# Pairwise attention pooling: one block per loop body on TensorE, a ring of three PSUM slots with x in it, and x scaled by GpSimd

## What is computed

```python
row, col = np.triu_indices(F, k=1)
ip = x[:, row, :] * x[:, col, :]
hidden = jax.nn.relu(jnp.einsum('bpd,da->bpa', ip, W_w) + b_w)
logits = jnp.einsum('bpa,a->bp', hidden, W_h) + b_h[0]
a = jax.nn.softmax(logits, axis=1)[:, :, None]
pooled = jnp.sum(a * ip, axis=1)
return pooled @ W_p + b_p
```

## Time and profile before

| | |
|---|---|
| median of 3 runs | 1325.57 us (1322.91 to 1327.94) |
| the profiled execution, own time | 1334.73 us |
| its span, first to last instruction | 1332.9 us |
| mean granted TensorE clock | 0.951 of 2.4 GHz |
| TensorE / VectorE / ScalarE / GpSimd busy | 87% / 70% / 71% / 22% |
| TensorE's instructions | 25856 matmuls, 25856 weight loads |
| mean data rate of the DMAs | 36 GB/s |

### The profile page before, as it was taken

One profiled execution on the slowest core, in us unless ns is written; L12 is line 12 of the kernel. 1 busy time (PEld: TensorE's weight loads), 2 busy tenths in 40 slices (PEclk: granted clock), 3 DMA queues, 4 the chain that ended last, 5 costly groups with the idle time before them and its releaser, 6 DMA issues.

```text
span 1332.9 us, 60251 instructions
## 1 busy us (share of the span) xinstructions
PE 1156.1 (87%) x25856; PEld 517.9 (39%) x25856; DVE 934.6 (70%) x484; ACT 951.3 (71%) x1123; POOL 286.6 (22%) x263
## 2 busy tenths in 40 slices
PE   7988979789787997979979889797997979979984
PEld 3433434334343443434433344333443434434432
DVE  8686667866678675876867767577686776867870
ACT  5776767767677686767857678576785767857873
POOL 3131221212122131221302213032130221312220
PEclk9998989999899998989989899898998989989998
DMA  3142132312423123241222412324122241412312
GB/s 51 30 46 34 28 41 35 47 28 28 41 39 40 31 31 39 39 48 22 33 36 39 49 21 32 37 39 49 21 37 34 37 49 21 48 30 33 46 20 22
DMA packets 333436, 47.63 MB, mean 36 GB/s; under 512 B 333280, under 2 KB 333280, under 8 KB 333280
## 3 DMA queue, kind: packets, MB, share of 16 engines
q1 hardware_dynamic: 331264, 45.16, 26.6%
q10 hardware_dynamic: 2016, 0.01, 0.1%
HBM read 26.59 MB, written 18.54 MB: 34 GB/s over the span
## 4 chain that ended last, share of the span: by engine, by line
PE 85%; issue 12%; ACT 1%; DMA 1%; SPq 1%; ACTq 0%; DVE 0%; DVEq 0%
PE z L481 52%; PE logits L501 25%; PE z L452 4%; PE x_cols L439 3%; ACT hidden L356 1%; PE logits L491 1%; DMA values<-gram 0%; DMA gram<-gram_out 0%; DMA bp_col<-in_L_rec_b_p_dram 0%; SPq L188 0%; ACTq L398 0%; SPq L176 0%; SPq L174 0%; ACTq L392 0%; ACTq L393 0%
## 5 line engine op out<-in xcount | busy, mean ns | idle before, releaser
L356 ACT ACTIVATE hidden<-z,b_col 128x988 f32<-128x988 f32 x768 | 815.1, 1083 | 319.2 <-PE z L481 308.2
L277 DVE TENSOR_TENSOR prod<-x_wide 128x2964 f32<-128x2964 f32 (+1 forms) x257 | 821.7, 3242 | 96.7 <-PE z L481 89.1
L481 PE MATMUL z<-prod,w_tiles 64*32 64x494 f32 x12288 | 833.9, 590 | 4.6 <-ACT hidden L356 2.8
L501 PE MATMUL logits<-hidden,head_w 64*32 64x371 f32 (+1 forms) x8192 | 489.6, 491 | 33.9 <-issue 33.4
L236 POOL COPY head_w<-head_cols 128x64 f32<-128x64 f32 x252 | 277.0, 1099 | 1007.8 <-PE logits L501 1004.6
L481 PEld LDWEIGHTS z<-prod,w_tiles 64*32 64x32 f32 x12288 | 234.0, 108 | 325.6 <-issue 254.1
L501 PEld LDWEIGHTS logits<-hidden,head_w 64*32 64x32 f32 x8192 | 197.7, 109 | 279.3 <-issue 271.8
L259 DVE COPY x_wide<-x_cols 128x624 f32<-128x624 f32 (+1 forms) x64 | 51.4, 804 | 246.1 <-PE x_cols L439 244.1
L340 ACT ACTIVATE x_scaled<-x_wide,wp_col 128x156 f32<-128x156 f32 x256 | 105.9, 414 | 1.2 <-DMA bp_col<-in_L_rec_b_p_dram 1.2
L491 PE MATMUL logits<-w_tiles 64*32 64x2 f32 x256 | 8.3, 185 | 96.3 <-issue 96.3
L452 PE MATMUL z<-x_wide,x_scaled 64*39 64x39 f32 x4096 | 56.5, 202 | 20.6 <-issue 20.6
(11 more groups left out here) (16 smaller groups left out, 14.6 us busy)
## 6 DMA issues: line engine op xcount, KB each, us to landing
x_rows<-in_r_x_dram SPq DMA_DIRECT2D x128, 156.0 KB
gram<-gram_out SPq DMA_DIRECT2D x256, 47.5 KB
gram<-gram_out SPq DMA_DIRECT2D x256, 23.2 KB
values<-gram SPq DMA_DIRECT2D x128, 46.3 KB, 3.6
w_tiles<-in_L_rec_W_w_dram SPq DMA_DIRECT2D x4, 16.0 KB, 2.5
head_cols<-in_L_rec_W_h_dram ACTq DMA_DIRECT2D x4, 0.2 KB, 3.8
out_dram<-y_all SPq DMA_DIRECT2D x4, 1.0 KB, 3.4
out_dram<-y_all ACTq DMA_DIRECT2D x4, 1.0 KB, 4.3
```

The lines of the kernel that those rows point to most:

```text
L277: nc.vector.tensor_tensor(out, one, other, ALU.mult).then_inc(ready, 1)
L356: nc.scalar.activation(hidden[:, i, :, CHUNK * k:CHUNK * (k + 1)], z[:, (slot + item(j)) % 2, :, 0:CHUNK], ACT.Relu, bias=b_col[:, 0:1]).t ...
L481: last = nc.tensor.matmul(z[col:col + TILE, at, b, 0:CHUNK], w_tiles[row:row + D, col:col + TILE], prod[row:row + D, i, first:first + CHUN ...
L501: last = nc.tensor.matmul(logits[TILE * q:TILE * (q + 1), part, 0:cols], head_w[row:row + A, e, b, :], hidden[row:row + A, e, b, first:fir ...
```

## The change

**TensorE's loops.** `two_blocks` is gone. The inner loop's body is one block and runs four times in a group; behind the outer loop, a loop of one block runs twice, and the last two blocks are written out.

**PSUM.** `z` has three slots. Besides the 12 chunks and the gram matrices, the transposed x goes through the ring too: 14 items in fixed slots that are the same in each block (`SLOT`, `X_SLOT`, `GRAM_SLOT`), and `EARLIER` says for each chunk which item it takes the slot from. `x_cols` is gone.

**SBUF.** `x_rows` and `x_wide` have one slot instead of two. So `load(v)` waits until x of v - 1 has been transposed, and the spread of a block waits for the gram matrices of the block before, which read `x_wide`.

**Scaling.** GpSimd scales x in one instruction a block, ahead of the block's four head copies; ScalarE no longer does.

**Start.** SP loads both halves of x first, then the weights; it also takes the six small DMAs for the head weights and the two scalars from ScalarE's queue, and `load(1)` comes behind them.

The diff, cut to its core:

```diff
-    SLOTS = 2
+    SLOT = (2, 1, 0, 2, 1, 0, 0, 1, 0, 2, 1, 0)
+    EARLIER = (9, 10, 11, 0, 1, 2, 5, "gram", 6, "x", 7, 8)
+    X_SLOT, GRAM_SLOT, FIRST_X_SLOT = 2, 1, 0
+    BEFORE_X, BEFORE_GRAM = 3, 4
...
-        x_rows = sb("x_rows", [ROWS, SLOTS, 2 * ROW_DUOS, D])
-        x_wide = sb("x_wide", [P, SLOTS, BLOCK_DUOS, WIDE])
+        x_rows = sb("x_rows", [ROWS, 2 * ROW_DUOS, D])
+        x_wide = sb("x_wide", [P, BLOCK_DUOS, WIDE])
...
-        z = ps("z", [P, 2, 2, BANK])
+        z = ps("z", [P, 3, 2, BANK])
         logits = ps("logits", [P, 2, BANK])
-        x_cols = ps("x_cols", [P, 2, BANK])
...
-            def load(v, slot):
+            def load(v):
+                sp.wait_ge(x_cols_ready, v + 1)
...
-                        sp.wait_ge(x_cols_ready, v + 2)
-                        load(v + 2, m % SLOTS)
+                        load(v + 2)
...
+            def scale_x(v):
+
+                pool.wait_ge(x_spread, 2 * (v + 1))
+                if v == 0:
+                    pool.wait_ge(act_spread, 2)
+                    pool.wait_ge(cols_loaded, 16 * N_COLS)
+                else:
+                    pool.wait_ge(z_ready, ITEMS * (v - 1) + CROSS_AT + 1)
+                nc.gpsimd.tensor_scalar(x_scaled[:, :, :], x_wide[:, :, 0:FIELDS], wp_col[:, 0:1], None,
+                                        ALU.mult).then_inc(x_scaled_ready, 1)
...
             for step in range(BLOCK_STEPS, STEPS):
+                if step % BLOCK_STEPS == 0:
+                    scale_x(step // BLOCK_STEPS)
                 place_heads(step)
...
-            def spread(v, slot, first=False):
+            def spread(v, first=False):
 
-                if not (isinstance(v, int) and v < SLOTS):
-                    dve.wait_ge(prod_ready, BLOCK_STEPS * (v - 1))
+                if not first:
+                    dve.wait_ge(prod_ready, BLOCK_STEPS * v)
+                    dve.wait_ge(z_ready, ITEMS * (v - 1) + CROSS_AT + 1)
                 dve.wait_ge(x_cols_ready, 1 if first else v + 2)
...
-                    if j == 1 and not (isinstance(v, int) and v == 0):
-                        scale_x(v, slot, 3)
-                    if more and j in (6, 7, 10):
-                        scale_x(v + 1, 1 - slot, (6, 7, 10).index(j))
...
+            def claim_slot(v, j, with_x):
+
+                earlier = EARLIER[j]
+                if earlier == "gram":
+                    pe.wait_ge(z_read, ITEMS * v + CROSS_AT + 1)
+                elif earlier == "x":
+                    if with_x:
+                        pe.wait_ge(x_spread, 2 * (v + 2))
+                elif earlier < j:
+                    pe.wait_ge(z_read, ITEMS * v + item(earlier) + 1)
...
-            def two_blocks(n):
-                block_work(2 * n, 0, n + 1)
-                block_work(2 * n + 1, 1, n + 2)
...
-                with pe.Fori(0, GROUP_BLOCKS // 2) as w:
-                    two_blocks(GROUP_BLOCKS // 2 * g + w)
+                with pe.Fori(0, GROUP_BLOCKS) as m:
+                    block_work(GROUP_BLOCKS * g + m)
...
-            two_blocks(BLOCKS // 2 - 2)
-            block_work(BLOCKS - 2, 0)
-            block_work(BLOCKS - 1, 1, following=False)
+            with pe.Fori(BLOCKS - GROUP_BLOCKS, BLOCKS - 2) as v:
+                block_work(v)
+            block_work(BLOCKS - 2, with_x=False)
+            block_work(BLOCKS - 1, following=False)
```

More of the change, by code:

```diff
@@ L147, in bass_pairwise_attention_pooling @@
         y_stored = sem("y_stored")
[L149 removed]
+        N_COLS = 4
+        N_SCALARS = 2
         GRAM_DMAS = 8
@@ L194, in _ @@
                     sp.dma_start(w_tiles[h * D:(h + 1) * D, c * A:(c + 1) * A], w_hidden).then_inc(w_loaded, 16)
-            sp.dma_start(x_rows[D:D + FIELDS, 0, :, :], x_rows_dram[1, :, 0, :, :]).then_inc(first_x_loaded[1], 16)
-            load(1, 1)
+            sp.wait_ge(zeroed, 1)
+            for h in range(2):
+                for b in range(2):
+                    at = GROUP_STEPS - 1 + GROUP_STEPS * (h ^ b)
+                    sp.dma_start(head_cols[h * D:(h + 1) * D, b, at:at + 1],
+                                 w_logit.rearrange("(a o) -> a o", o=1)).then_inc(head_cols_loaded, 16)
+            for col, scalar in ((bh_col, b_logit), (bp_col, b_out)):
+                sp.dma_start(col[:, :],
+                             scalar.rearrange("(a o) -> a o", o=1).broadcast_to((P, 1))).then_inc(scalars_loaded, 16)
+            load(1)
             def group(g, pairs, last=False):
@@ L279, in find_max @@
             def find_max(g):
+                if isinstance(g, int) and g == 0:
+                    dve.wait_ge(scalars_loaded, 16 * N_SCALARS)
                 dve.wait_ge(logits_done, GROUP_STEPS * (g + 1))
@@ L297, in pool_group, with block_work @@
                                         ALU.mult, ALU.add).then_inc(y_ready, 1)
-            def block_work(v, slot, pooled_group=None, ended=None, more=True):
-                multiply(v, slot, 0)
+            def block_work(v, pooled_group=None, ended=None, more=True):
+                multiply(v, 0)
                 if pooled_group is not None:
@@ L304, in block_work @@
                 for i in range(1, BLOCK_STEPS):
-                    multiply(v, slot, i)
+                    multiply(v, i)
                 if ended is not None:
@@ L334, in _, with rectify @@
         def _(act):
[L335 to L341, removed]
             def spread_first():
                 act.wait_ge(x_cols_ready, 2)
-                cols = x_cols[:, 1, 0:XCOLS].rearrange("p (q f) -> p q f", f=FIELDS)
-                wide = x_wide[:, 0, ROW_DUOS:BLOCK_DUOS, :]
+                cols = z[:, FIRST_X_SLOT, 1, 0:XCOLS].rearrange("p (q f) -> p q f", f=FIELDS)
+                wide = x_wide[:, ROW_DUOS:BLOCK_DUOS, :]
                 nc.scalar.copy(wide[:, :, 0:FIELDS], cols).then_inc(act_spread, 1)
                 nc.scalar.copy(wide[:, :, FIELDS:WIDE], cols[:, :, 0:OFFSETS]).then_inc(act_spread, 1)
-            def rectify(v, slot, j):
+            def rectify(v, j):
                 i, k = j // THIRDS, j % THIRDS
@@ L375, in exponentials, with block_work @@
                                      accum_out=exp_sum[:, :]).then_inc(logits_free, 1)
-            def block_work(v, slot, writes, ended=None, more=True):
+            def block_work(v, slot, writes, ended=None):
                 for j in range(CHUNKS):
-                    rectify(v, slot, j)
+                    rectify(v, j)
                     if j == CROSS_AT - 1:
@@ L425, in _ @@
                 v = BLOCKS - GROUP_BLOCKS + m
-                block_work(v, m % SLOTS, v // 2, ended=GROUPS - 2 if m == 0 else None, more=m < GROUP_BLOCKS - 1)
+                block_work(v, m % 2, v // 2, ended=GROUPS - 2 if m == 0 else None)
             exponentials(GROUPS - 1)
@@ L472, in hidden_layer @@
                     pe.wait_ge(prod_ready, BLOCK_STEPS * v + i + 1)
-                if not (isinstance(v, int) and v == 0 and j < 2):
-                    pe.wait_ge(z_read, ITEMS * v + item(j) - 1)
+                claim_slot(v, j, with_x)
                 nc.tensor.sem_inc(z_claimed, 1)
-                at = (slot + item(j)) % 2
                 for a in range(0, A, TILE):
```

142 lines of the change are left out of this document (64 added, 78 removed).

## The result

The changed kernel takes 1100.55 us (median of 4 runs, 1099.71 to 1101.29) against 1326.76 us (4 runs, 1322.91 to 1328.64): a ratio of 0.830, 95% interval 0.828 to 0.832.

The account below looks back on a forecast made before the run. TensorE's own time and its issue time (code fetches) bound the kernel. Sum 19.3 + 956.5 + 4.5 + 68.3 + 55.9 + 26.0 = 1130.5 us span, 1132 profiled, forecast 1128; range 1108 to 1190 us.

Parts of the forecast that it names:

- the profiled run: Profiled execution before lay 9.2 us above the median of the runs; half was taken off, 1132 to 1128 us.
- the fetches: TensorE's outer return reads its code again; a one-block body would not, saving 14.2 us in each of 14 groups.
- Three slots: Chunk gated by the reading three places before instead of two: gains nothing, as undisturbed blocks have TensorE busy 16.99 of 17.01 us.
- the stalls of a first pass: TensorE's first reading of code, with stalls and slow clock: 4.5 us kept in the first group, 6.4 at the end.
- the ring: Slots of z that chunks and x share: third slot gains nothing, new waits for x and its spread not on the path.
- the group's end: Opening of the logits between TensorE's groups: 0.27 us without a fetch, some 0.2 us of it on the chain.
- the scaling: Scaling x moves from ScalarE to GpSimd: worth 0, off the path; GpSimd's instruction taken as 1.0 us, bounds 0.81 and 2.3.
- The rival of GpSimd and VectorE: The two hinder each other, x_scaled or the spread comes late, TensorE waits 1 us a block: 1192 us, chance 0.09.
- the port: GpSimd's scaling may begin only after VectorE's first multiplication, done 3.2 + 1.0 us after the spread; needed some 14 us after.
- the outer return still misses: Rival: TensorE's outer return still fetches its code, 12.3 us at each of 14 returns, 172 in all: 1300 us, chance 0.07.
- every return fetches: Rival: TensorE's inner returns fetch too, 7.1 us for each of 46, plus 172 us: 1627 us, chance 0.03.
- The start: Load order and ScalarE's six DMAs before the first chunk: bounds -4 and +3 us, taken as -2.

Follow-up runs that it names:

- e2: Kernel before, with the opening of the logits done two more times ahead of TensorE's outer loop (64 instructions, executed once): 1134.2 us, ratio 0.861.
- e8: Changed kernel with two copies of the block in TensorE's inner body, shifted by 64 instructions: 1097.9 us, ratio 0.834 to the kernel before.
- e9: Kernel before, with the opening of the logits done six more times ahead of TensorE's outer loop (192 instructions, executed once): 1473.9 us, ratio 1.118.
- e4: Changed kernel, each chunk gated by the item two places before it, though it has three slots: 1127.9 us, ratio 0.857 to the kernel before.
- e6: Changed kernel with two copies of the block in TensorE's inner body and each chunk gated two items before: 1315.4 us, ratio 0.999 to the kernel before.
- e1: Changed kernel with two copies of the block in TensorE's inner body, run twice a group: 1241.8 us, ratio 0.944 to the kernel before.
- e3: Changed kernel with x scaled by ScalarE in four pieces between the chunks, not by GpSimd: 1099.8 us, ratio 0.834 to the kernel before.

## Why the prediction was right and wrong

| term, us | predicted | measured |
|---|---|---|
| to the first logit half | 19.3 | 18.9 |
| fifteen groups | 1029.3 | 1004.7 |
| last three blocks to the last gram matrix | 55.9 | 48.5 |
| DMAs and pooling at the end | 26.0 | 26.8 |
| around the span, and from the profiled run to the median | -2.8 | +1.6 |
| sum | 1128 | 1100.5 |

**Right: the fetches.** The reading of the earlier trace rows, a store that holds the two-block body but not head, body and the piece ahead, passed in e2 and e8 (19 and 16 pieces in all), and e9's count of nine pieces a missed return fits it too. The largest term, 14 groups at 14.2 us, was removed as forecast; e2 took out 183 us by it alone, near the 196 us (14 x 14 us) expected there. That the store keeps more than what was read last is shown by e8: it returns 29 times over more than six pieces (1689 instructions and more, at 256 a piece) and fetches 16 in all. The reading was incomplete, though: it laid the overflow on the size of the code. Head and body are 1726 instructions in the trace, and with a piece of 256 they are 1982, where eight pieces have 2048. They overflow only where the code straddles borders so that it lies in eight pieces; e2 and the kernel before differ in this alone. The changed kernel's 883 instructions, opening and one block, lie in five pieces at most, wherever the borders fall.

**Wrong: "Three slots ... so this gains nothing".** This is the step that failed. I read "busy 16.99 of 17.01 us" as full use. e4 shows that the third slot gives 27 us: 0.39 us a block, 63 times, and some 3 us in the first group. The evidence was in the trace of before: pairs of chunks at 1.77 us beside single ones at 0.83. (The mean matmul of a chunk, 590 ns before and 576 after, says less than it seems to: in e2, with the old ring but without the stretches at a granted clock of 0.50, it is 579.)

**Wrong: the stalls of a first pass.** I kept 4.5 us for the first group and 6.4 for the end, 10.9 in all, by the rule that straight reading costs what it cost before. After, both are near nothing: the first group is as long as the second, and the end is 48.5 us against 48.0 for its pieces. e4 and e6 show that these stalls hang on the gate: with the gate of two, e4's first group has 2.9 us too much. So the ring, priced at nothing, failed here a second time.

**Mis-sized the other way: the group's end.** I took 0.2 us; a group is 66.9 us against 66.2 for four blocks: 0.7 us, 15 times, some 7 us more than forecast. The chain has 0.22 us for the opening, 0.28 us of issue behind it, and a first logit half of 0.86 us in place of 0.62. The gap of 0.26 us behind the opening stood in the earlier trace rows, and I had set it aside for the returns. I took the price from the last opening of the kernel before, behind which straight code follows; there the gap is missing. Between two groups, where the inner loop follows, it is there with or without a fetch. Whether it belongs to entering that loop is not shown: the trace names ScalarE's copy of the gram matrices as the releaser in some groups, and no run separates the two.

**Mis-sized: the profiled run.** It lay 9.2 us above the median before, and 0.1 us above it after. I had kept half.

**Right in effect, wrong in size: the scaling.** VectorE and GpSimd in order of time, changed kernel:

```profile
152.73 3.25 DVE L310 TENSOR_TENSOR prod<-x_wide 128x2964 f32<-128x2964 f32 x1
155.90 1.43 DVE L325 CUSTOM_DVE_ANT_0 weighted<-exps,values 128x742 f32<-128x742 f32 x1
...
169.91 13.31 DVE L310 TENSOR_TENSOR prod<-x_wide 128x2964 f32<-128x2964 f32 x4
185.15 0.81 DVE L292 COPY x_wide<-z 128x624 f32<-128x624 f32 x1 [1.93 <-PE z L453]
...
152.70 4.91 POOL L263 TENSOR_SCALAR x_scaled<-x_wide,wp_col 128x624 f32<-128x624 f32 x1 [2.98 <-DVE x_wide L293]
```

The scaling is issued beside the multiplication and ends 1.6 us after it: 1.6 us of its own, for 1.0 taken and 0.81 to 2.3 as bounds. By the profile it takes 4.91 us, more than the 4.3 named as the most to be seen. What comes next on VectorE is held up by 0.5 us (1.43 for 0.93 us, and 13.31 us for four multiplications that took 12.79), so VectorE's round is 14.6 us, and it idles 1.93 us before the next spread. The spread ends 0.5 us or so into the next block; TensorE's waits for VectorE are 2.4 us in the whole run, at the start. The rival of GpSimd and VectorE was real as a delay on these two engines, but cost TensorE nothing.

What the prediction calls the port is in the traces this: of the 256 head copies of the kernel before, 162 start inside a multiplication, and each of them ends 0.09 to 0.10 us after the end of one, in all 0.28 to 3.26 us long; the other 94 take 0.24 us at most. What the two engines share, no trace names. Nor is the hold total: the multiplication that starts at 173.08 us, before the scaling of that block ends at 174.79, takes 3.74 us for the 3.25 of the one before it, so it loses 0.5 us and not the 1.6 us for which the scaling goes on. And that much of a copy's 0.24 us is fixed fits GpSimd's memsets at the start of the kernel before, 0.10 us for one column and 0.13 us for 39: some 0.10 of the 0.24 us, as an estimate from these.

**The rivals.** That the outer return still misses was refuted by the changed kernel itself: five of its 13 pieces are read by 40 us, and none from there to 1020 us. That every return fetches is refuted for it by the same count, but comes true in e9: there every return of the kernel before fetches, and it is slower by 157 us, 10.5 for each of 15 inner returns where the rival had 7.1. The cause there is where the code lies, and not a store that keeps only what was read last.

## What to carry to other kernels

Where a program on TensorE loops, look at the instruction queue by stretch, and at whether a return reads its code again: what decided in these runs is whether everything between the farthest head and the end, plus one piece ahead, lies within eight pieces of 16 KB (256 instructions each in these traces), and that depends on where the first piece's border falls. In e2 and e8 it did, and 19 and 16 pieces were read in all; in the kernel before and in e9 it took nine, and 145 and 281 were read. Sixty-four instructions put ahead of a loop were worth 183 us here, 192 cost 157. And a busy engine is not a fast one: compare the duration of the same work at two places of a block before calling a wait hidden.

## What the runs showed of the hardware that was not expected

- The kernels that fetch code in their loops scatter somewhat more: before, 1309 to 1329 us in all its runs, e6, e9 and e1 over 10, 9 and 7 us, against 1.6 us for the changed kernel and up to 6 for the others without such fetches.
- A return that misses costs more than its two or three stalls. In e9's inner return a stall of 4.6 us is followed by a first logit half of 1.49 us for 0.86, with a granted clock of 0.50 from 159 to 162 us; two blocks with one missed return come to 44.0 and 48.5 us for 34.
- With a gate of two items in place of three, TensorE's pieces of code are asked for 24 to 72 matmuls later (e6 against e1). Where code was being fetched, that gate cost 3.3 us a group, and 2.9 us in the only such group of e4, on top of what it cost otherwise.
- Of all parts of the change, the body of one block, the ring's room and the place of the scaling, two are worth most of the time: 183 to 187 us for the fetches (e2, and e6 to e4), 27 us for the ring. The start gives some 2 us, by the first logit half at 18.9 us for 21.3; no run takes it back alone. e8 and e3 do as well as the changed kernel within what the runs can tell.
